# A two-layer decoder on one core: the last attention's weights times values in four column groups, a transposed gate, and routing placed between an expert's matmuls

## The reference

```python
h = rmsnorm(x, ln1_w)                       # x: the normalised residual, 1024 x 128
q, k, v = h@Wq+bq, h@Wk+bk, h@Wv+bv         # 16 query heads, 4 key/value heads of width 8
q, k = rmsnorm(rope(q), qn_w), rmsnorm(rope(k), kn_w)
attn = softmax(causal(q @ k.T / sqrt(8)))   # per head, 1024 x 1024
out = attn @ v                              # 1024 x (16*8)
gate = sigmoid(out @ Wg + bg)               # Wg, bg: 8 x 8 and 8, the same for each head
x = x + (out * gate) @ Wo + bo
h2 = rmsnorm(x, ln2_w)
top1 = argmax(h2 @ Wr + br)                 # one of 8 experts
u = h2 @ W1[e] + b1[e]; act = u[:, :256] * sigmoid(u[:, 256:])
y = act @ W2[e] + b2[e]                     # taken for e = top1
return x + y                                # added to the decoder's residual
```

## Time and profile before

| | us |
|---|---|
| median of 3 runs (lowest, highest) | 1891.41 (1890.3, 1895.34) |
| the profiled execution, its own time | 1896.19 |
| its span, first to last instruction | 1894.4 |
| PE busy | 1526.4 (81%) |
| DVE busy | 1318.5 (70%) |
| ACT busy | 926.9 (49%) |
| POOL busy | 697.9 (37%) |

### The profile page before, as it was taken

How to read it: one execution, slowest core, us unless ns; L and a number is a source line. 1 busy time by engine, 2 the same in 40 slices (tenths; PEclk the granted TensorE clock), 3 DMA queues, 4 the chain that set the end, 5 groups by cost and what they waited for, 6 DMA issues and landing times. The chain is left out here.

```text
span 1894.4 us, 20029 instructions
## 1 busy us (share of the span) xinstructions
PE 1526.4 (81%) x6681; PEld 814.2 (43%) x6737; DVE 1318.5 (70%) x3033; ACT 926.9 (49%) x1448; POOL 697.9 (37%) x526
## 2 busy tenths in 40 slices
PE   5776998999867468788878878887574399999798
PEld 2223443455435124455445545555453233333555
DVE  5997677565274599989999899898474646664233
ACT  5664114656213117777777777788211045554121
POOL 1765111121000008887888888788200200000012
PEclk8898999999878678998989898898777579999599
DMA  5000110000092200000000000000200200000000
GB/s 134 1 1 13 51 51 3 1 1 0 17 199 45 58 0 1 1 1 1 1 1 1 1 1 1 1 1 1 84 8 16 72 1 1 1 1 1 0 1 11
DMA packets 30244, 37.14 MB, mean 20 GB/s; under 512 B 13543, under 2 KB 23371, under 8 KB 29007
## 3 DMA queue, kind: packets, MB, share of 16 engines
q1 hardware_dynamic: 28586, 23.96, 4.6%
q10 hardware_dynamic: 1544, 11.79, 3.1%
HBM read 29.50 MB, written 6.24 MB: 19 GB/s over the span
## 5 line engine op out<-in xcount | busy, mean ns | idle before, releaser
L1472 PE MATMUL psum<-film_ka,film_context_qa 97*128 97x512 bf16 (+1 forms) x832 | 342.7, 413 | 145.7 <-DVE search_and_weigh_kept L1667 64.0
L1844 ACT ACTIVATE search_and_weigh_e<-psum,search_and_weigh_bias 128x512 f32<-128x512 f32 (+1 forms) x416 | 268.0, 666 | 111.2 <-PE psum L1474 107.3
L1667 DVE MAX8 search_and_weigh_kept<-psum 128x8 f32<-128x171 f32 (+2 forms) x1216 | 317.7, 324 | 5.0 <-PE psum L1474 3.8
L1474 PE MATMUL psum<-film_kb,film_context_qb 128*128 128x512 bf16 (+1 forms) x777 | 318.2, 410 | 0.0
L1693 DVE SCALAR_TENSOR_TENSOR search_and_weigh_e<-psum,film_context_top,search_and_weigh_e 128x512 f32<-128x512 f32 (+1 forms) x283 | 201.0, 717 | 37.5 <-ACT search_and_weigh_e L1844 35.1
L1715 POOL TENSOR_TENSOR search_and_weigh_e<-search_and_weigh_e,search_and_weigh_keep 128x512 f32<-128x512 f32 (+1 forms) x133 | 150.7, 1133 | 167.9 <-ACT search_and_weigh_keep L1823 165.0
L1472 PEld LDWEIGHTS psum<-film_ka,film_context_qa 97*128 97x128 bf16 x832 | 92.2, 111 | 253.4 <-DVE search_and_weigh_e L1693 99.2
L2678 DVE TENSOR_REDUCE gqa_attend_low<-psum 128x1 f32<-128x128 f32 (+7 forms) x128 | 96.6, 757 | 84.2 <-PE psum L2602 83.8
L2889 POOL TENSOR_TENSOR residual<-residual,top_expert_kept 128x1024 f32<-128x1024 f32 x8 | 18.7, 2344 | 357.1 <-DVE top_expert_kept L2862 357.1
L1749 PEld LDWEIGHTS psum<-ctx_rows,search_and_weigh_mean_T 128*128 128x128 f32 (+1 forms) x816 | 131.8, 207 | 32.8 <-issue 6.0
L1719 POOL TENSOR_TENSOR search_and_weigh_mean<-search_and_weigh_e 128x512 f32<-128x512 f32 (+1 forms) x104 | 134.1, 1290 | 12.3 <-DVE search_and_weigh_e L1693 5.1
(11 more groups left out here) (551 smaller groups left out, 2767.2 us busy)
## 6 DMA issues: line engine op xcount, KB each, us to landing
film_kb<-film_k_rows ACTq DMA_DIRECT2D x4, 1601.0 KB
film_ka<-film_k_rows ACTq DMA_DIRECT2D x3, 1601.0 KB
ctx_T<-in_ctx_T SPq DMA_DIRECT2D x1, 2401.5 KB
gqa_experts_w<-in_L_ffn_W SPq DMA_DIRECT2D x1, 2048.0 KB
film_convolve_back<-in_dft_back SPq DMA_DIRECT2D x1, 1728.0 KB, 13.1
film_k_rows<-cross_attention_film_hi SPq DMA_DIRECT2D x6, 256.0 KB, 2.0
film_k_rows<-cross_attention_film_mid SPq DMA_DIRECT2D x6, 256.0 KB, 2.0
film_k_rows<-cross_attention_film_low SPq DMA_DIRECT2D x6, 256.0 KB, 2.0
```

Source lines behind the costliest of these rows:

```text
L1472: pe.matmul(out, a["qa"][0:ROWS, h, rows], a["ka"][0:ROWS, h, c + b:c + b + cols], start=True, stop=False)
L1474: last = pe.matmul(out, a["qb"][:, h, rows], a["kb"][:, h, c + b:c + b + cols], start=False, stop=True)
L1667: last = dve.max(kept[:, h % 2, first + s, :], bank[:, lo:hi])
L1844: act.activation(e[:, n % RING, sub, 0:PIECES[u][1]], ps[:, SEARCH_BANKS + q % WEIGH_BANKS, 0:PIECES[u][1]], ACT.Exp, bias=bias[:, i % 2, ...
```

## The change

It does five things.

1. `outputs` is called every second step with two key tiles. Tile parity and half choose the column group, so that one head takes all four: its call for tiles k and k+1 issues up to four matmuls to four groups. Even and odd tiles have sums of their own, which DVE adds: it copies 64 partitions of bank 7 to `stack` and adds the other 64 (L2669, L2670 of the new kernel). The next head waits for this one's addition (before: the head after next for both copies). DVE clears bank 7 once before the first head. `stack` has 8 x 512 columns for 4 x 1024, and POOL's clearing of it is gone.
2. `gqa_output` normalises two heads at a time, with two instructions of each kind for the two halves of the tokens. The gate is made transposed: `w_g` is the stationary operand, the result needs no turning, and `b_g` is the sigmoid's bias. `b_o` is added by DVE to `xn`. The one-row bias matmuls are gone, halves of 512 are handed on separately.
3. `top_expert` starts the first expert right behind h's transposes; the logits come behind its first unit (`CHOOSE_AT`), the choice's transposes behind its second, the `b2` matmuls behind the third (`BIAS_AT`). `b_r` is added by DVE.
4. The last expert's result is kept, added by DVE (not POOL) and stored in two halves, within the block; the stage `store_output` is gone.
5. `b_g`, `b_o` and `b_r` are loaded as a column and as rows for all partitions.

```diff
-            link(pool.memset(a["stack"][:], 0.0))
...
-                if k == 0 and h >= 2:
-                    pe.wait_ge(o_ready, 2 * (h - 1))
+                if k == 0:
+                    if h == 0:
+                        pe.wait_ge(out_zeroed, 1)
+                    else:
+                        pe.wait_ge(o_ready, h)
                 for half in range(2):
-                    lo, hi = max(k * P, half * HALF), (half + 1) * HALF
...
+                    for kk in (k, k + 1):
+                        lo, hi = max(kk * P, half * HALF), (half + 1) * HALF
+                        if lo < hi:
+                            last = pe.matmul(out_quadrant(kk, half)[:, lo - half * HALF:HALF],
+                                             a["v"][:, kk, h // (HQ // HKV), :],
+                                             prob[:, h % 2, kk, lo - kk * P:hi - kk * P],
+                                             start=kk < 2, stop=hi - (kk + 1) * P < 2 * P,
+                                             tile_position=(0, 32 * (2 * (kk % 2) + half)))
...
-                    outputs(h, k)
+                if 0 <= h < HQ and k % 2:
+                    outputs(h, k - 1)
...
-                    for half in range(2):
-                        dve.tensor_copy(a["stack"][32 * (h % 4):32 * (h % 4) + OUT, h // 4,
-                                                   half * HALF:(half + 1) * HALF],
-                                        out_quadrant(h, half)).then_inc(o_ready, 1)
+                    rows = a["stack"][64 * (h % 2):64 * (h % 2) + 64, h // 2, :]
+                    link(dve.tensor_copy(rows, out_rows(0)))
+                    dve.tensor_tensor(rows, rows, out_rows(1), ALU.add).then_inc(o_ready, 1)
...
-                pe.matmul(out, oT[:, i * P:(i + 1) * P], w_g[:], start=True, stop=False)
-                pe.matmul(out, g["ones"][:, 0:P], b_g[:], start=False, stop=True).then_inc(gate_done, 1)
-            transpose_tiles(pe, gated, g["ident"][:], ps[:, 4:6, :], gated_ready, gT_psum)
+            for n in range(2):
+                pe.wait_ge(oT_ready, n + 1)
+                pe.matmul(ps[:, 2 + n, :], w_g[:], oT[:, n * HALF:(n + 1) * HALF], start=True,
+                          stop=True).then_inc(gate_done, 1)
...
-            for k in range(HQ // 4):
+            for k in range(HQ // 2):
                 dve.wait_ge(turned, k + 1)
...
+                for n in range(2):
+                    dve_share = dve.reciprocal(share[:, 4 * n:4 * n + 4, heads], out[:, n, :, :, HD])
+                link(dve_share)
...
+                    if 2 * e + q == CHOOSE_AT:
+                        route()
+                    if 2 * e + q == CHOOSE_AT + 1:
+                        turn_own()
+                    if 2 * e + q == BIAS_AT:
+                        own_bias()
...
+            for n in range(2):
+                rows = slice(4 * n, 4 * n + 4)
+                link(dve.tensor_tensor(kept[:, e % 2, rows], ps[:, 6 + n, :].rearrange("p (i d) -> p i d", d=D),
+                                       own[:, rows, e:e + 1].to_broadcast([P, 4, D]), ALU.mult))
+                dve.tensor_tensor(g["x"][:, rows], g["x"][:, rows], kept[:, e % 2, rows],
+                                  ALU.add).then_inc(result, 1)
...
+            for n in range(2):
+                sp.wait_ge(result, n + 1)
+                sp.dma_start(out[:, 4 * n:4 * n + 4], g["x"][:, 4 * n:4 * n + 4]).then_inc(stored, 16)
```

More of the change, by code:

```diff
@@ L2354, in gqa_experts @@
 def gqa_experts(nc, g, t, m):
[L2357 removed]
+    a = {"xn": m.sb("xn", [P, NT, D]), "stack": m.sb("stack", [P, HQ // 2, HALF])}
     a["weights"] = {n: m.sb(n, s) for n, s in (
[L2360 to L2361 removed]
+        ("w_g", [P, D]), ("b_g", [P, 1]), ("w_o", [P, D]), ("b_o", [P, D]),
+        ("ln_w", [P, 1]), ("w_r", [P, NE]), ("b_r", [P, NE]), ("order", [P, NE]),
         ("w1", [P, NE, 2 * EH]), ("b1", [P, NE, 4]), ("w2", [P, NE, 2, D]), ("b2", [NE, D]))}
@@ L2739, in _ @@
         def _(pe):
-            for k in range(HQ // 4):
-                for i in range(NT):
-                    last = pe.transpose(ps[:, 2 * k + i // 4, (i % 4) * P:(i % 4 + 1) * P],
-                                        a["stack"][:, k, i * P:(i + 1) * P], g["ident"][:])
+            for k in range(HQ // 2):
+                for i in range(4):
+                    last = pe.transpose(ps[:, k, i * P:(i + 1) * P], a["stack"][:, k, i * P:(i + 1) * P],
+                                        g["ident"][:])
                 last.then_inc(turned, 1)
-            pe.wait_ge(o_ready, HQ // 4)
+            pe.wait_ge(o_ready, HQ)
             for i in range(NT):
@@ L2886, in _ @@
             pool.wait_ge(bias_read, 1)
-            for e in range(NE):
+            for e in range(NE - 1):
                 pool.wait_ge(y_read, e + 1)
@@ L2899, in _ @@
                                scale=ln_w[:, 0:1]).then_inc(hT_ready, 1)
-            act.wait_ge(oT_psum, 1)
-            act.activation(own_T[:], pair(3)[0:NE, :], ACT.Copy).then_inc(oT_ready, 1)
             for e in range(NE):
@@ L2909, in _ @@
                                    bias=b1[:, e, 2 + q:3 + q]).then_inc(sig_ready, 1)
+                    if n == CHOOSE_AT + 1:
+                        act.wait_ge(oT_psum, 1)
+                        act.activation(own_T[:], pair(3)[0:NE, :], ACT.Copy).then_inc(oT_ready, 1)
         @block.tensor
@@ L2913, in _, with route, turn_own @@
             transpose_tiles(pe, h, g["ident"][:], ps, h_ready, hT_psum)
-            for i in range(NT):
-                pe.wait_ge(hT_ready, i // 4 + 1)
-                out = ps[:, 2, i * NE:(i + 1) * NE]
-                pe.matmul(out, hT[:, i * P:(i + 1) * P], w_r[:], start=True, stop=False)
-                last = pe.matmul(out, g["ones"][:, 0:P], b_r[:], start=False, stop=True)
-            last.then_inc(logit_done, 1)
-            def own_bias():
+            def route():
+                for i in range(NT):
+                    last = pe.matmul(ps[:, 6, i * NE:(i + 1) * NE], hT[:, i * P:(i + 1) * P], w_r[:], start=True,
+                                     stop=True)
+                last.then_inc(logit_done, 1)
+            def turn_own():
                 pe.wait_ge(sum_ready, 1)
@@ L3035, in decoder @@
         Memory.used.clear()
-        for part in PARTS + [store_output]:
+        for part in PARTS:
             with ExitStack() as ctx:
```

141 lines of the change are left out of this document (72 added, 69 removed).

## The result

The changed kernel takes 1829.78 us (median of 4 runs, 1822.18 to 1832.86), the kernel before 1891.81 in the runs beside it. The ratio is 0.9664, with a 95% interval of 0.9631 to 0.9696. It is faster; the forecast of 1836 was 6 us too high, the range of 1816 to 1854 holds the result. The profiled execution has a span of 1831.1 us for 1894.4, so 63.3 less for a predicted 55.5.

A forecast was written before the change was run, and what follows sets the result against it. PE bounds attention's steady stretch; `gqa_output` is a chain where one engine works. Attention -27.5, clearing -1.6, `gqa_output` -14.1, routing -11.0, end -1.3 sum to -55.5: 1840.7 us profiled, 1836 against the median, range 1816 to 1854.

The forecast's parts named there:

- Four groups side by side: Attention's weights times values: four column groups run together as two do, 3.3 us off a head's PE work.
- The stalls that come back: Attention: PE waits again for ACT (1.2 us) and DVE's shift (0.4), 1.6 a head, leaving heads of 11.3 us.
- POOL's clearing: `gqa_project`: without POOL's clearing of `stack`, a small DVE instruction no longer waits for it, -1.6 us.
- The division: `gqa_output`: 32 small DVE instructions at 0.25 us make 8.0 us, starting 0.5 earlier, +4.1 us.
- Behind the division: `gqa_output`: the chain after the division takes 9.9 us at half-clock prices for 28.1, 18.2 less; full clock 3 more.
- Routing: `top_expert`: first expert starts 15.7 us earlier, routing groups between units add 4.7, net -11.0 us (-6 to -11).
- The end: After the last matmul: DVE additions and store in halves take 6.0 to 7.0 us for 7.8, -1.3 us.
- pairs only: Rival in attention: four groups run only two at a time, +12 us, 1848 in all; chance 0.14.
- nothing overlaps: Rival in attention: no column groups run side by side, attention 22 us longer, total 1886; chance 0.04.
- no stalls: Rival in attention: the waits do not come back since ACT and DVE keep up on average, 1810; chance 0.09.
- a drop spread over the heads: Rival in attention: PE's gaps make the clock drop at times, granted 0.91, +15 us, 1851; chance 0.19.
- the low clock for all of attention: Rival: PE stays at half clock in attention, heads of 19.4 us, 1966 with all sixteen; chance 0.03.

The follow-up runs named there:

- two-group run: Changed kernel with weights times values on two column groups instead of four, calls still merged by twos: 1865.6 us, ratio 0.9855 to the kernel before.
- the lags: Four runs of the changed kernel with attention's steps (query turn, shifted-score turn, exponentials, outputs) moved against each other, no instruction added or removed: 1818.7 to 1825.4 us.
- serial run: Changed kernel with a wait behind each small VectorE instruction of the division: 1836.5 us, ratio 0.9686 to the kernel before.
- lags 7, 11, 13, 14: Changed kernel with queries turned at step 7, shifted scores at 11, exponentials from 13, outputs from 14: 1821.0 us, ratio 0.9607 to the kernel before.
- gate as before: Changed kernel with the old gate and output projection in `gqa_output`, one-row bias matmuls and second turn included: 1849.5 us, ratio 0.9754 to the kernel before.

## Why the prediction was right, and where it was not

- **Four groups side by side** held to the hundredth: a call in 1.04 us for a predicted 1.03. The two-group run shows that this, and not fewer calls, is the gain. The Trainium skill's 2.38 times for three column tiles ("TensorE: Matmul & The Clock Gate", Part 3: Packing small matmuls) gave, as an estimate for four, full calls of 1.2 us; the trace does not agree, it has 1.04.
- **The stalls that come back.** 1.6 us a head predicted, as half of the 3.3 that could come back. A head of 11.19 less the 9.7 of PE work priced from the rows gives 1.5; the rows name 0.8 (8.9 us in 120), and 0.93 is what order alone removed. That order makes PE stand is shown by the lags; the size lies between 0.93 and 1.5, and how it divides between ACT and DVE (1.2 and 0.4 predicted) stays open. No row had said half, so that it came this close is in part luck. Attention gained 28.7 us for a predicted 27.5.
- **POOL's clearing**: -1.8 for -1.6, shown by putting it back.
- **The division** is the term that was mis-sized: +0.8 for +4.1. The step that failed is "One costs 0.23 or a little less and 0.03 between two". The serial run gives that price (8.63 us); neighbours without a wait between them overlap. The Trainium skill ("VectorE: DVE Perf Modes", Two Vector instructions with no wait between them) says that such an instruction may start before the one ahead has finished, unless one of its conditions holds it back; the trace agrees, 0.27 us for two against 0.45.
- **Behind the division** the step "by prices of the half clock, since PE idles for these 8 us" failed. The division took 5.4 us, the clock stayed at full until 1728.2, and the chain cost 7.5 us for 9.9. That the division was shorter than thought does not explain it: in the serial run it took 8.6 us, and the chain behind still only 8.2, with 3.4 us at half clock. The working had the other case too: "at full clock 3 more". With the division, the stage gained 19.8 us for 14.1, which is most of what the forecast missed.
- **Routing**: -9.9 for -11.0. The wait ahead went as predicted. The groups between the units cost about 5 us (80.9 less the 76.0 that 78.1 would be without its 4.2 us at half clock), close to 4.7. What was missed is the clock: I had it rise four us into the experts as before, and it rose 6.2 us in, which costs 1.0. This moves from run to run: with lags 7, 11, 13, 14 it rose 4.8 us in.
- **The end**: -2.3 for -1.3. From the last matmul's end it took 5.5 us, under the 6.0 to 7.0 that was worked out. The four VectorE instructions took 2.74 us for 2.9, and the landing of 256 KB 2.3, near the 2.0 row and not the 3.2 of 512 KB. No run isolates this one.
- **Rivals**: pairs only, nothing overlaps and no stalls are refuted. The clock did fall in attention, but only in the tail of the last head, for 3.4 us; in the steady stretch it is 1.00, so a drop spread over the heads is refuted. So is the low clock for all of attention: it rose at 1540.4, 27.7 us behind attention's start for 25.4 before.

All misses but the routing's point the same way: 3.3 + 2.5 + 1.2 + 1.0 - 1.1 = 6.9. The clearing, the layer norm and the 0.6 us ahead of the last part, which the change does not touch, make up the rest of the 7.8 us between 55.5 and 63.3, rounding aside.

## What to carry to other kernels

When a bound engine's work is cut, ask which waits its work was covering, and price the schedule as well as the work: here a quarter less PE work gave back at least 0.9 us a head to standing, and four constants recovered that much. Price the stages behind a change at both clock levels, and look at what PE does in the gaps: the same rest left the first expert's matmuls at half clock when it was empty (6.08 us) and at full clock when it was filled (3.70). Small instructions in a row should have no waits between them unless one reads what the other wrote.

## What the runs showed of the hardware

- Matmuls with 9 output rows, fp32, up to 512 columns: 8 records to four column groups took 1.04 us, to two groups 1.89.
- Two VectorE instructions of 8 elements with no wait between them took 0.27 us, with one 0.45; two of 64 elements 0.36 and 0.48.
- A VectorE instruction on 8 elements took 1.89 us while POOL cleared 128x4096, and ended within 0.1 us of it; 0.17 without the clearing.
- A 128-column fp32 matmul with a new weight costs 0.25 us at full clock (eight `b2` ones in 1750.42 - 1748.45 = 1.97), but where each alternates with a one-row matmul the two cost 0.84 (1717.98 - 1717.14), 0.42 apiece.
- The granted clock fell to half while such pairs ran without a gap, 5.5 us after they began (gate as before) and 2.9 us (kernel before). It stayed at full over the layer norm once four 512-column matmuls stood in PE's 5.3 us of rest.
